# Splitting the softmax maxima: a copy and a two-input subtraction become two one-input reductions

## The reference

```
scores = jnp.einsum('bqhd,bkhd->bhqk', Q, K) / np.sqrt(HEAD_DIM)
attn = jax.nn.softmax(scores, axis=-1)
attn_out = jnp.einsum('bhqk,bkhd->bqhd', attn, V).reshape(B, N, D_MODEL)
attn_out = attn_out @ Wo + bo
```

## Time and profile before

| what | value |
|---|---|
| median of 3 runs | 376.14 us (375.49 to 376.29) |
| the profiled execution, whole time | 374.76 us |
| its span in the trace | 372.9 us |
| PE busy | 362.0 us (97%) |
| DVE busy | 328.1 us (88%) |
| ACT busy | 316.3 us (85%) |
| POOL busy | 186.8 us (50%) |
| granted TensorE clock | 0.995 of full speed |

### The profile page before, as it was taken

The page is one execution under the profiler, slowest core; times in us unless marked ns, Lnnn a source line. Parts: engine busy times, 40 slices in busy tenths (PEclk is TensorE's granted clock), DMA queues, the critical chain, the costliest instruction groups (busy, mean ns, idle before and its releaser), DMA issues.

```text
span 372.9 us, 10415 instructions
## 1 busy us (share of the span) xinstructions
PE 362.0 (97%) x3706; PEld 205.7 (55%) x3707; DVE 328.1 (88%) x768; ACT 316.3 (85%) x632; POOL 186.8 (50%) x290
## 2 busy tenths in 40 slices
PE   8999899999999999999999999999999999999987
PEld 3634444546655554555556545464645564456876
DVE  6389999999899989899999899999999999963663
ACT  6304688999999898998999889999989999998784
POOL 5435999676497223784024681205861031104874
PEclk9989999999999999999999999999999999999999
DMA  7810257211004100005000023000041000000002
GB/s 227 237 41 15 58 147 182 75 60 35 2 16 130 32 2 6 0 21 156 3 6 3 0 77 97 4 2 6 2 125 49 2 3 4 3 3 3 1 1 58
DMA packets 17187, 17.64 MB, mean 47 GB/s; under 512 B 2460, under 2 KB 15454, under 8 KB 17120
## 3 DMA queue, kind: packets, MB, share of 16 engines
q1 hardware_dynamic: 15840, 16.19, 15.8%
q10 hardware_dynamic: 1296, 0.79, 0.9%
HBM read 6.62 MB, written 0.52 MB: 19 GB/s over the span
## 4 chain that ended last, share of the span: by engine, by line
PE 65%; DVE 7%; POOL 3%; issue 2%; ACT 1%; DVEq 0%; ACTq 0%; POOLq 0%
PE pv_ps L849 19%; PE max_ps L663 11%; PE exp_ps L672 10%; PE max_ps L796 7%; PE exp_ps L783 6%; DVE mx L1150 5%; PE exp_ps L632 2%; PE max_ps L632 2%; PE exp_ps L718 2%; PE max_ps L653 2%; POOL rstd L1171 1%; PE max_ps L754 1%; PE exp_ps L834 1%; PE exp_ps L653 1%; ACT probs L974 1%
## 5 line engine op out<-in xcount | busy, mean ns | idle before, releaser
L1150 DVE TENSOR_REDUCE mx<-max_ps 128x1 f32<-128x512 f32 x384 | 240.6, 681 | 4.9 <-PE max_ps L663 3.6
L974 ACT ACTIVATE probs<-exp_ps 128x512 f32<-128x512 f32 x384 | 201.0, 603 | 11.5 <-PE exp_ps L672 10.6
L663 PE MATMUL max_ps<-k_stack,q_stack 64*128 64x512 bf16 x384 | 111.6, 385 | 2.4 <-DVE mx L1150 0.8
L849 PE MATMUL pv_ps<-probs,v_ones 128*32 128x256 f32 x1536 | 103.1, 385 | 0.0
L672 PE MATMUL exp_ps<-q_stack,k_stack 64*128 64x256 bf16 x768 | 99.3, 272 | 0.0
L1170 POOL TENSOR_SCALAR var_eps<-mv 128x2 f32<-128x2 f32 (+2 forms) x33 | 6.4, 194 | 146.8 <-DVE mv L1008 146.2
L849 PEld LDWEIGHTS pv_ps<-probs,v_ones 128*32 128x32 f32 x1536 | 43.4, 109 | 32.4 <-issue 9.2
L672 PEld LDWEIGHTS exp_ps<-q_stack,k_stack 64*128 64x128 bf16 x768 | 41.6, 94 | 29.2 <-ACT probs L974 12.5
L663 PEld LDWEIGHTS max_ps<-k_stack,q_stack 64*128 64x128 bf16 x384 | 32.1, 94 | 45.6 <-DVE mx L1150 28.2
L986 ACT ACTIVATE mrows<-exp_ps 8x256 bf16<-8x256 bf16 x48 | 17.4, 364 | 13.6 <-PE exp_ps L834 13.5
L783 PE MATMUL exp_ps<-hT,w 128*128 128x256 f32 x96 | 26.7, 397 | 0.0
(11 more groups left out here) (128 smaller groups left out, 492.5 us busy)
## 6 DMA issues: line engine op xcount, KB each, us to landing
k_stack<-parts SPq DMA_DIRECT2D x36, 128.0 KB, 2.5
q_stack<-parts SPq DMA_DIRECT2D x30, 128.0 KB
w<-in_w_dram SPq DMA_DIRECT2D x4, 448.0 KB, 3.9
w<-in_w_dram SPq DMA_DIRECT2D x4, 256.0 KB, 3.0
w<-in_ada_dram SPq DMA_DIRECT2D x1, 896.0 KB, 5.4
w<-in_rows_dram SPq DMA_DIRECT2D x1, 832.0 KB, 8.8
q_stack<-mrows SPq DMA_DIRECT2D x48, 4.0 KB
x<-in_x_dram SPq DMA_DIRECT2D x2, 256.0 KB, 3.5
```

The costliest lines, as they stand in the source:

```text
L663: return pe.matmul(max_bank(n), half(q_stack, b, pair, j)[:, t * P:(t + 1) * P], half(k_stack, b, pair, j), start=True, stop=True)
L849: mm = pe.matmul(pv_ps[32 * j:32 * j + 32, cols_of(g // 2)], v_ones[:, b, kt, 4 * g + j, :], probs[:, (4 * i + j) % RING_P, cols_of(of_two ...
L974: act.activation(probs[:, tile % RING_P, :], exp_bank(e), ACT.Exp, scale=SCORE_SCALE[hc // 2 // NB]).then_inc(exp_read, 1)
L1150: dve.tensor_reduce(mx[:, G % 2, t, 2 * (pair % 2) + j:2 * (pair % 2) + j + 1], max_bank(n), AX_X, ALU.max, negate=True).then_inc(max_read, 1)
```

## The change

`mparts` goes. `mx` becomes a float32 tile of 64 words a partition, with an axis of two for "value" and "parts". The maximum is now written with its own sign. `SPLIT` is two `tensor_reduce` of one input each. The first copies each maximum, negated and rounded to bfloat16, into the upper half of a float32 word whose lower half is zero, so that the word read as float32 is the negated rounded part. The second adds value and that word over an axis of length two, negated, and writes float32. The transpose on PE reads the upper halves of the words, at a step of two bfloat16 elements. One `memset` of the 64 words is added at the start of DVE's program.

The waits are moved as well. `SPLIT` of group G no longer waits for the rows of group G - 2; instead the first `MAX` of group G (there is one for each of the two heads of a pair, so two instructions carry it) waits for them, in the place of the wait for `max_split`.

```
-        mx = sb("mx", [P, 2, TH, 4])
-        mparts = sb("mparts", [P, 2, TH, 4, 2], BF16)
+        mx = sb("mx", [P, 2, 2, TH, HALVES, 2, 2])
...
-                        mm = pe.transpose(out[0:8, t * P:(t + 1) * P], mparts[:, G % 2, t].rearrange("p a b -> p (a b)"), ident_bf[:, :])
+                        both_parts = mx[:, G % 2, 1, t].rearrange("p j part a -> p (j part a)").bitcast(BF16)[:, 1::2]
+                        mm = pe.transpose(out[0:8, t * P:(t + 1) * P], both_parts, ident_bf[:, :])
...
             dve.memset(warm[:, :].bitcast(F32), 0.0).then_inc(first_tile_set, 1)
+            dve.memset(mx[:, :, :, :, :, :, :], 0.0)
             dve.memset(half[:, 4:5], 0.0).then_inc(zeros_set, 1)
...
-                    m, pt = mx[:, G % 2].rearrange("p t (a j) -> p t j a", j=HALVES), mparts[:, G % 2]
+                    upper = mx[:, G % 2, 1].rearrange("p t j part a -> p (t j) (part a)").bitcast(BF16)[:, :, 1::2]
                     for j in range(HALVES):
                         dve.wait_ge(*read_by_dve(("MAX", G // GROUPS, GROUP_BEATS * (G % GROUPS) + GROUP_BEATS - 1, j)))
-                    if G >= 2:
-                        dve.wait_ge(*read_by_act(("ROWS", G - 2, 0, 0)))
-                    settle(dve.tensor_reduce(pt[:, :, 1:3, :], m.unsqueeze(4), AX_X, ALU.max))
-
-                    dve.tensor_tensor(pt[:, :, 0::3, :], m, pt[:, :, 1:3, :], ALU.subtract).then_inc(max_split, 1)
+                    settle(dve.tensor_reduce(upper[:, :, 2:4], mx[:, G % 2, 0, :, :, 1].rearrange("p t j a -> p (t j) a").unsqueeze(3), AX_X, ALU.max, negate=True))
+                    dve.tensor_reduce(mx[:, G % 2, 1, :, :, 0].rearrange("p t j a -> p (t j) a"), mx[:, G % 2, :, :, :, 1].rearrange("p both t j a -> p (t j) a both"),
+                                      AX_X, ALU.add, negate=True).then_inc(max_split, 1)
...
                     if G >= 2 and m % GROUP_BEATS == 0:
-                        dve.wait_ge(max_split, G - 1)
+                        dve.wait_ge(*read_by_act(("ROWS", G - 2, 0, 0)))
                     dve.wait_ge(max_full, FULL[n])
-                    dve.tensor_reduce(mx[:, G % 2, t, 2 * (pair % 2) + j:2 * (pair % 2) + j + 1], max_bank(n), AX_X, ALU.max,
-                                      negate=True).then_inc(max_read, 1)
+                    dve.tensor_reduce(mx[:, G % 2, 0, t, j, 1, pair % 2:pair % 2 + 1], max_bank(n), AX_X, ALU.max).then_inc(max_read, 1)
```

## The result

The changed kernel takes 379.87 us in the median of six runs (379.04 to 381.06), beside 375.75 us for the kernel before, six runs on the same chip: 1.0117 times as long, with a 95% interval of 1.0099 to 1.0136. It is slower by about 4.4 us, where 1.1 us had been forecast, and the median lies 0.9 us above the range. So the two profiled spans differ by 6.3 us, the medians by 4.1 us: with places in the two traces one accounts for the 6.3 us, with the medians of experiments for the 4.1 us. Of all executions reported here one, of `before_fetch_earlier` (380.48 us), was in a slower state of the chip and is left out of the ratios.

The account below looks back on a forecast made before the run. DVE was taken as the bound from 26 to 88 us, PE from 88 to 331 us. Cost 3.8 less gain 2.7 made +1.1 us on the median of 376.14: 377.2 us, range 374.2 to 379.0 us.

Parts of the forecast that it names:

- Step 1: First reduction of the split on DVE: 151 ns like the old one, no difference; at most 1.8 us of DVE.
- Step 2: Second reduction of the split on DVE: 159 ns against 167, a gain of 0.1 us where DVE is the bound.
- Step 3: Split's meetings with POOL on DVE vanish: 4.27 us of DVE, of which 1.23 and 1.34 us reach the end.
- Steps 4 and 5: PE's strided transpose load: nothing, up to 1 us at the far end; DVE's starting memset: 0.07 us, hidden.
- Step 6: Moved wait at first maxima of groups 12, 13, 19, 21, 37: DVE held 5.03 us, 3.8 reaching the end.
- E: Rival: reductions on SBUF meet POOL too, the gain goes and the cost stays: +3.8, 379.9 us; chance 0.02.
- D: Rival: DVE's waits cost all their length and grow, holding the next group too: +3.5, 379.6 us; chance 0.08.
- A: Rival: DVE's waits are absorbed by up to three PSUM banks, the gain stands: 374.4 us; chance 0.28.

Follow-up runs that it names:

- before_fetch_earlier: The kernel before with 45 more idle waits in PE's queue at the start, to bring an instruction fetch into the copies for group 40: 375.48 us, 1.0002.
- two_inputs: `ops_only` with the second reduction replaced by one operation of two SBUF inputs, layout, memset and strided load kept: 375.82 us, 1.0016.
- ops_only: The changed kernel with the wait for the rows of G - 2 put back to `SPLIT`, new operations kept: 375.06 us, 0.9992 of the kernel before.
- late_21: The changed kernel with the wait at the first maximum only in group 21, at the split elsewhere: 376.0 us, 1.0013 of the kernel before.
- wait_only: The kernel before with its old operations, only the wait moved from the split to the group's first maximum: 380.16 us, 1.0118.
- ops_fetch_later: `ops_only` with 223 idle waits added to PE's queue at the start, to move instruction fetches behind the copies: 381.06 us, 1.0152.

## Why the prediction was wrong in size and right in sign

**Step 1, first reduction.** 161 ns in the median instead of 151: 48 x 10 ns = 0.5 us of DVE. `Nothing` was too low; the 37 ns kept as the other end held it.

**Step 2, second reduction.** 173 ns, not 159, and 6 ns more than the 167 ns of the operation that it replaced: no gain of 0.1 us, but a loss of the same size. (Ten of the 48 splits lie where DVE is the bound, a fifth and not a third.) Both steps together add 16 ns a split, 0.8 us of DVE in all. The Trainium skill's rule (VectorE: DVE Perf Modes, "Rules for kernel authors") was right in direction here, tensor_reduce is the slower one, but by 6 ns of 167, and the operation's freedom from POOL is worth far more. The slope of 1.07 ns a value, drawn from PSUM reads of 512 values, was too flat for 16 values: 8 more took 12 ns beside the new first reduction and 22 beside the old.

**Step 3, the meetings with POOL.** The mechanism holds, as `two_inputs` shows, and the Trainium skill's section (SBUF — State Buffer, "Who interferes with whom") agrees with the trace: 750 ns with two SBUF inputs, at most 176 ns with one. The terms held too as long as one looks at their place: 0.8 us between 26 and 88 us instead of 1.23, and in the account's steps at the three places on the chain 0.52, 0.33 and 0.53 us instead of 0.52, 0.33 and 0.49. What failed is the sum that took them to the end. A lead won ahead of a start of a chain is largely lost there, so 2.7 us of forecast gain were 0.3 us in `ops_only`, and 0.3 to 1.1 us in all four measurements. This is 1.6 to 2.4 us of the error. The prediction took what stood on the chain of the kernel before for what reaches the end; it did not ask what else a chain's first tile waits for once DVE is early, the copies behind POOL's split and the fetches beside them.

**Steps 4 and 5.** The strided load takes 86 instead of 85 ns, and nothing of DVE's start is later by the memset. Both right.

**Step 6, the moved wait.** The holds were found and sized from the trace of before, as idle time of DVE: 1.27, 0.83, 0.82, 1.33 and 0.45 us against 1.33, 0.91, 0.90, 1.39 and 0.50, in sum 4.70 against 5.03. All five are where they were named, and no sixth one is there. What failed is the share that reaches the end. The forecast had 3.8 of 5.03, with 1.0 of 1.39 at group 21, 1.7 of 2.24 at 12 and 13 and 0.2 of 0.5 at 37. The account shows each of them passed on at full length at once, group 37 included (+0.58). Medians give 4.4 to 4.8 us for the five. That is 0.6 to 1.0 us of the error. For one hold alone, `late_21`, the share of the forecast would have been about right: 0.8 us of 1.33, to within 0.9. PE's rows fit this: of its waits for DVE's maxima the kernel before had 0.8 us, the changed one 2.2 us and `wait_only` 3.0 us. And PE's weight loads for score tiles waited for DVE 76 times in the kernel before already (total us, times, longest):

```profile
PEld max_ps L663 <- DVE mx L1150: 28.2, 76, 0.8
...
PE max_ps L663 <- DVE mx L1150: 0.8, 3, 0.4
```

Three banks are no cushion where DVE is already three banks behind.

**The rivals.** By the number E came nearest, 379.9 us, given 0.02, and that is luck: it had the reductions meet POOL, which `two_inputs` and the 176 ns refute. What it shares with the result is that the gain is missing at the end, for another reason. D, 379.6 us, given 0.08, is right in its first half, the waits cost all their length at their places. Its second half, that holds grow, did not happen: each is slightly shorter than read before. A, that the banks absorb the holds, is refuted by `wait_only`.

**The two errors point the same way**, 1.6 to 2.4 us of gain that vanished and 0.6 to 1.0 us of cost that was discounted. Together 2.2 to 3.4 us, and the medians ask for 4.4 - 1.1 = 3.3. The profiled executions ask for more, 6.3 - 1.1 = 5.2 us; they are a fast one of the kernel before and the slowest of the changed one. In the latter the start of the chain at group 16 cost 1.55 us, of it a part in a single issue of SP: six copies take 5.92 us where the kernel before needed 4.19. SP's issues, after:

```profile
118.44 5.92 SPq L550 DMA_DIRECT2D q_stack<-parts  x6
```

The last of the six, from 122.03 to 124.36 us, stood beside a fetch from 122.18 to 123.99 us. `wait_only`, whose six copies took 4.19 us, still lost 0.97 us at group 16, so the long issue is not the only way: there the fetch began at 123.16 us, 0.21 us ahead of the last issue's end, and the copy landed in 3.12 instead of 2.58 us. No run removes this fetch and leaves all else, so its share of the 0.97 us isn't known.

## What to carry to other kernels

Before an engine's wait is moved forward in its queue, list for each use when the awaited work ends and when the waiting instruction starts: the holds read in this way were right to 0.1 us, and where the engine that waits for the held one has no slack they are to be charged in full at their place; a wait that stands later anyway may take a part of them up again. A gain on an engine that is not the bound must be followed to the next place where something else starts the work, here the copies of a new chain, and it counts only as far as that other thing moves too. Two edits in one change, an operation and a wait, should be timed apart: here the one is worth 0.3 to 1.1 us and the other costs more than 4, and with the wait left where it was the version is as fast as before or faster. Before a lead is read from two single traces, one looks whether the granted clock was the same in both.

## What the runs showed of the hardware

- A DVE operation with two SBUF inputs is held by POOL's also as scalar_tensor_tensor: 169 ns in the median, 750 ns at most; a reduction with one input over the same data took 172 to 176 ns in all of 48 cases.
- An instruction fetch of 16 KB took 0.9 to 2.4 us (391 of them in the 13 traces). Where one began 0.8 us or less behind the last of the copies for group 40, they landed 2.82 to 3.38 us after that issue, instead of 1.91 us where none did.
- An issue of a 128 KB copy on the SP queue takes 0.6 us; beside a fetch of 16 KB it took up to 2.34 us. 32 of the 39 issues of over 1.0 us ended 0.29 to 0.44 us after such a fetch.
- Waits that are already fulfilled cost time in PE's queue: with 14 of them ahead of each, the first sixteen products of `ops_fetch_later` start 0.78 us apart instead of 0.43, so a wait costs at most 0.055 us. Not all of the 8.9 us are these waits: the last products behind them still start 0.43 us apart, where in `ops_only` they start 0.22 us apart.
- The granted clock of TensorE fell to 0.50 from 19.9 to 23.3 us in the profiled execution of the kernel before, and not at all there in that of `ops_only`; DVE was 0.85 us later for it at 26 us.
